# Routed experts on 256-row tiles of dispatched tokens instead of all tokens through every expert

## What is computed

```
x = x + _layernorm(attn(_layernorm(x)))          # 16 heads of 64, causal, relative bias
x = x + _layernorm(moe(_layernorm(x)))
# moe, xf is [2048, 128]:
shared = new_gelu(xf @ Wfc_s + bfc_s) @ Wproj_s + bproj_s        # 128 -> 512 -> 128
probs = softmax(xf @ Wr); topk_p, topk_i = top_k(probs, 2)
topk_p = topk_p / sum(topk_p)
for e in range(8):
    h = new_gelu(xf @ Wfc[e] + bfc[e]) @ Wproj[e] + bproj[e]
    routed = routed + h * gate[:, e:e + 1]                       # gate is 0 for 6 of 8 experts
```

## Time and profile before

| | |
|---|---|
| median of 3 runs | 844.47 us (841.37 to 845.34) |
| the profiled execution: its time | 844.46 us |
| its span | 842.7 us |
| PE busy | 771.5 us (92%) |
| DVE busy | 707.7 us (84%) |
| ACT busy | 612.8 us (73%) |
| POOL busy | 298.9 us (35%) |
| DMA moved | 70.72 MB |

### The profile page before, as it was taken

One profiled execution on the slowest core, in us unless ns is written; L12 is line 12 of the kernel. 1 busy time (PEld: TensorE's weight loads), 2 busy tenths in 40 slices (PEclk: granted clock), 3 DMA queues, 4 the chain that ended last, 5 costly groups with the idle time before them and its releaser, 6 DMA issues.

```text
span 842.7 us, 17198 instructions
## 1 busy us (share of the span) xinstructions
PE 771.5 (92%) x4436; PEld 657.1 (78%) x4436; DVE 707.7 (84%) x1596; ACT 612.8 (73%) x1340; POOL 298.9 (35%) x323
## 2 busy tenths in 40 slices
PE   3877999999999999999999999996489999999992
PEld 2656988888888888888889888885377777777771
DVE  5557888988888888888888888888778888898976
ACT  2356888887888888888788888873577767667672
POOL 2318823333332332333233233223503354445423
PEclk9899999999999999999999999999679999999997
DMA  7684334424423432442443343230003211122101
GB/s 279 219 280 89 75 66 97 88 62 87 100 62 76 95 77 62 93 94 62 87 95 67 70 97 82 62 75 26 25 1 129 76 60 43 46 75 75 51 1 50
DMA packets 56025, 70.72 MB, mean 84 GB/s; under 512 B 36032, under 2 KB 45120, under 8 KB 52544
## 3 DMA queue, kind: packets, MB, share of 16 engines
q1 hardware_dynamic: 55712, 69.83, 32.9%
q10 hardware_dynamic: 288, 0.59, 0.3%
HBM read 27.36 MB, written 9.50 MB: 44 GB/s over the span
## 4 chain that ended last, share of the span: by engine, by line
PE 75%; DVE 8%; issue 6%; POOL 4%; ACT 3%; DMA 3%; POOLq 0%; DVEq 0%; ACTq 0%; SPq 0%
PE out_ps L1191 16%; PE score_ps L1158 16%; PE trans_ps L1173 15%; PE shared_ps L1205 6%; PE trans_ps L1074 3%; PE score_ps L1074 3%; PE score_ps L1076 2%; PE score_ps L1075 2%; PE trans_ps L1075 2%; PE trans_ps L1076 2%; DVE pT_lo L961 2%; PE shared_ps L1074 2%; PE shared_ps L1076 2%; PE shared_ps L1075 2%; POOL rstd L421 1%
## 5 line engine op out<-in xcount | busy, mean ns | idle before, releaser
L649 ACT ACTIVATE probs<-score_ps,row_min 128x128 f32<-128x128 f32 (+7 forms) x256 | 189.9, 742 | 53.5 <-DVE row_min L848 53.4
L861 DVE TENSOR_TENSOR pT_lo<-trans_ps,pT_hi 128x512 fp32r<-128x512 f32 (+3 forms) x384 | 201.6, 552 | 16.7 <-ACT pT_hi L670 16.6
L670 ACT ACTIVATE pT_hi<-trans_ps 128x512 fp32r<-128x512 f32 (+3 forms) x384 | 185.1, 491 | 40.4 <-PE trans_ps L1173 28.8
L848 DVE CUSTOM_DVE_ANT_0 score_ps<-score_ps,bias 128x128 f32<-128x128 f32 (+7 forms) x256 | 194.6, 760 | 22.8 <-PE score_ps L1158 19.4
L1173 PE MATMUL trans_ps<-ident,probs 128*128 128x128 f32 x1152 | 190.0, 274 | 3.2 <-DVE pT_lo L861 1.8
L1158 PE MATMUL score_ps<-k_hl,q_hl 128*128 128x512 f32 (+2 forms) x768 | 182.5, 351 | 3.1 <-DMA k_hl<-k_hl 1.6
L470 POOL TENSOR_TENSOR acc<-acc,head_out 128x512 f32<-128x512 f32 x64 | 83.0, 1297 | 245.5 <-DVE head_out L879 245.3
L1173 PEld LDWEIGHTS trans_ps<-ident,probs 128*128 128x128 f32 x1152 | 136.8, 140 | 27.3 <-DVE pT_lo L861 11.9
L1191 PE MATMUL out_ps<-pT_hi,v_hl 128*128 128x512 f32 (+2 forms) x384 | 156.5, 409 | 1.1 <-DVE pT_lo L861 1.1
L961 DVE TENSOR_TENSOR pT_lo<-probs,pT_hi 128x512 fp32r<-128x512 f32 x144 | 133.2, 952 | 25.0 <-ACT pT_hi L728 15.1
L1158 PEld LDWEIGHTS score_ps<-k_hl,q_hl 128*128 128x128 f32 x768 | 134.4, 189 | 23.7 <-DMA k_hl<-k_hl 1.8
(11 more groups left out here) (122 smaller groups left out, 1163.3 us busy)
## 6 DMA issues: line engine op xcount, KB each, us to landing
q_hl<-k_hl SPq DMA_DIRECT2D x64, 256.0 KB, 3.6
k_hl<-k_hl SPq DMA_DIRECT2D x32, 512.0 KB, 4.2
v_scratch<-probs SPq DMA_DIRECT2D x16, 512.0 KB, 4.0
v_raw<-v_scratch SPq DMA_DIRECT2D x32, 256.0 KB, 4.6
bias_all<-gate_scratch SPq DMA_DIRECT2D x8, 1024.0 KB, 4.8
v_raw<-in_Wfc SPq DMA_DIRECT2D x8, 256.0 KB, 4.9
bias<-in_Wproj SPq DMA_DIRECT2D x8, 256.0 KB, 5.3
bias_all<-in_rel_steps SPq DMA_DIRECT2D x1, 1920.0 KB, 12.7
```

Source lines behind the costliest of these rows:

```text
L649: act.activation(probs[s % 4][:, 0:n], scores_of(s % QB)[:, 0:n], ACT.Exp, bias=row_min[:, s:s + 1], scale=-1.0, accum_out=row_sum[:, s:s ...
L670: act.activation(pT_hi[c][:, CH * g:CH * g + m, q * P:(q + 1) * P], trans_ps[k % 2][:, 0:m * P].rearrange("p (m q) -> p m q", q=P), ACT.Co ...
L848: dve.tensor_tensor_reduce(out=ps, in0=ps, in1=bias_b[b][:, T - n:T], scale=1.0, scalar=3e38, op0=ALU.add, op1=ALU.min, accum_out=row_min[ ...
L861: dve.tensor_tensor(pT_lo[c][dst], trans_ps[k % 2][:, 0:m * P].rearrange("p (m q) -> p m q", q=P), pT_hi[c][dst], ALU.subtract).then_inc(p ...
```

## The change

The routed experts no longer see all tokens. Each of the 2048 tokens has two picks, so there are 4096 rows of work. They are sorted by expert into a list in DRAM, in which each expert's part is padded to whole tiles of 256 rows (TS = 256, NJ = 2 blocks of 128). In the worst case that needs 23 tiles, NT = 23, and all 23 are always run.

- **Weights.** The 16 weight matrices of the routed experts ("halves") are split into high and low parts during the heads, one in each head: SP loads a half (256 KB), POOL splits it (`split_half`, in slot 10), SP stores both parts (512 KB) to `split_scratch`.
- **An emptied list.** During head 0 ACT's queue fills the 5888 rows of `rows_scratch` with zeros and with harmless destinations. POOL writes the small tables for it (`make_tables`).
- **Places.** PE counts with 17 small matmuls how many tokens before each one chose the same expert (`ranks`), and DVE works out from that the first tile of each expert and the slot of each row, with 14 small instructions.
- **Dispatch.** POOL scatters the token rows to their slots with 32 indirect DMAs of 128 rows (`dispatch`), each row of 130 numbers: 128 of the token, its gate, and where its result goes.
- **Tiles.** For each tile SP reads the tile's expert number from SBUF into a register, waits, issues two weight loads of 512 KB and one small one (`load_weights`), and loads rows of the tile three ahead of the weights (`load_rows`). There are three weight buffers, six row buffers and two result buffers. PE turns the rows (`tile_in`), runs twelve matmuls of 256 columns (`tile_units`), twelve more (`tile_second`), and turns the result back (`tile_result`). DVE scales by the gate, and POOL scatters the two blocks of the result to `y_scratch` with two indirect DMAs (`store_tile`).
- **End.** When all results have landed SP loads both parts of every token's result, DVE adds them to the shared expert's result, and the output norm goes as before.

The multiplications by three, the attention and the shared expert are as they were.

The core of the diff. SP, where it loads for the tiles:

```
+            def load_weights(i):
+
+                e = sp.value_load(tile_expert_i[0:1, i:i + 1], min_val=0, max_val=E - 1)
+                if i >= 3:
+                    sp.wait_ge(yT_ready, i - 2)
+                for part in range(2):
+                    sp.dma_start(tile_w[i % 3][part].bitcast(f32),
+                                 bass.AP(split_dram.tensor, e * (2 * P * 2 * HID) + part * (P * 2 * HID),
+                                         [[2 * HID, P], [1, 2 * HID]])).then_inc(tile_w_loaded[i % 3], 16)
...
+            def load_rows(i):
+
+                if i >= NR:
+                    sp.wait_ge(y_stored[(i - NR) % 2], 16 * NJ * ((i - NR) // 2 + 1))
+                sp.dma_start(tile_rows[i % NR], rows_dram[i * TS:(i + 1) * TS, :].rearrange("(j p) r -> p j r", p=P))\
+                  .then_inc(tile_rows_loaded[i % NR], 16)
...
+            sp.wait_ge(half_stored, 16 * HALVES)
+            sp.wait_ge(scores_ready, H * S)
+            sp.wait_ge(table_ready, 1)
+            for i in range(3):
+                load_weights(i)
+            sp.wait_ge(dispatched, 16 * 2 * NB)
+            for i in range(NR):
+                load_rows(i)
+            for i in range(3, NT):
+                load_weights(i)
+                if i + NR - 3 < NT:
+                    load_rows(i + NR - 3)
+
+            for i in (NT - 2, NT - 1):
+                sp.wait_ge(y_stored[i % 2], 16 * NJ * (i // 2 + 1))
+            for c in range(NCH):
+                for k in range(2):
+                    lo = k * B * T + c * W
+                    sp.dma_start(y_part[k][:, CH * c:CH * (c + 1), :],
+                                 y_dram[lo:lo + W, :].rearrange("(t p) d -> p t d", p=P)).then_inc(y_loaded[c], 16)
```

SP and POOL in the heads, and POOL's scatters:

```
+                store_half(h)
+                if not last:
+                    load_half(h + 1)
...
+                if s == QB + 2:
+                    split_half(h)
...
+            def dispatch():
+
+                pool.wait_ge(slots_ready, 1)
+                pool.wait_ge(fields_ready, 1)
+                pool.wait_ge(rows_emptied, 32)
+                for i in range(2):
+                    for t in range(NB):
+                        pool.indirect_dma_start(rows_dram, bass.IndirectOffsetOnAxis(slot_u[i][:, t:t + 1], 0),
+                                                rows[i][:, t, :], None).then_inc(dispatched, 16)
+
+            def store_tile(i):
+
+                pool.wait_ge(y_ready, i + 1)
+                for j in range(NJ):
+                    pool.indirect_dma_start(y_dram, bass.IndirectOffsetOnAxis(tile_rows[i % NR][:, j, D + 1:D + 2].bitcast(u32), 0),
+                                            tile_out[i % 2][:, j, :], None).then_inc(y_stored[i % 2], 16)
```

PE's tile loop, and DVE's:

```
+            tile_in(0)
+            for i in range(NT):
+                tile_units(i)
+                if i + 1 < NT:
+                    tile_in(i + 1)
+                if i:
+                    tile_second(i - 1)
+                if i >= 2:
+                    tile_result(i - 2)
...
+            tile_in(0)
+            for i in range(NT):
+                tile_units(i)
+                if i + 1 < NT:
+                    tile_in(i + 1)
+                if i >= 2:
+                    tile_result(i - 2)
```

More of the change, by code:

```diff
@@ L386, in _ @@
[L386 to L397, removed]
+            sp.dma_start(wfc_raw, Wfc_s).then_inc(moe_w_loaded, 16)
@@ L1012, in _ @@
             for i in range(2):
-                then_wait(dve.tensor_tensor(top[i][:], top[i][:], first[:], ALU.mult))
-                then_wait(dve.tensor_tensor(pick[i][:], pick[i][:], each(top[i][:]), ALU.mult))
-            dve.tensor_tensor(gate[:], pick[0][:], pick[1][:], ALU.add).then_inc(gate_ready, 1)
-            gate_expert(0, 0, 0)
+                last = dve.tensor_tensor(rows[i][:, :, D], top[i][:], first[:], ALU.mult)
+            last.then_inc(fields_ready, 1)
+            shared_out(0)
@@ new lines, in _ @@
+            dve.tensor_copy(tile_expert_i[:], tile_expert[:]).then_inc(table_ready, 1)
+            then_wait(dve.scalar_tensor_tensor(out=place[:], in0=first_tile[:].unsqueeze(1).broadcast_to([P, NB, E]),
+                                               scalar=float(TS), in1=shared_ps[:, 0:NB * E].rearrange("p (t e) -> p t e", e=E),
+                                               op0=ALU.mult, op1=ALU.add))
+            for i in range(2):
+                then_wait(dve.tensor_tensor(place_of[:], place[:], pick[i][:], ALU.mult))
+                then_wait(dve.tensor_reduce(slot_f[i][:], place_of[:], AX, ALU.add))
+                last = dve.tensor_copy(slot_u[i][:], slot_f[i][:])
@@ L1047, in add_x @@
+            tile_result(NT - 2)
+            tile_result(NT - 1)
+            def out_moments(c):
+                lo, hi = CH * c, CH * (c + 1)
+                dve.wait_ge(y_loaded[c], 32)
+                dve.wait_ge(shared_ready, NCH)
+                for k in range(2):
+                    then_wait(dve.tensor_tensor(acc[:, lo:hi, :], acc[:, lo:hi, :], y_part[k][:, lo:hi, :], ALU.add))
+                moments(acc, lo, hi)
             def add_x(c):
@@ L1305, in transpose_gates, with ranks @@
-            def transpose_gates():
-                pe.wait_ge(gate_ready, 1)
-                for c in range(NCH):
-                    last = pe.transpose(out_ps[0:CH * E, c * P:(c + 1) * P],
-                                        gate[:, CH * c:CH * (c + 1), :].rearrange("p j e -> p (j e)"), ident[:])
-                last.then_inc(gate_T_psum, 1)
+            def ranks():
+                pe.wait_ge(picks_ready, 1)
+                pe.wait_ge(tables_ready, 1)
+                width = (NB + 1) * E
+                pe.matmul(shared_ps[:, 0:width], before_me[:], taken[:], start=True, stop=False)
+                for d in range(1, NB + 1):
+                    last = pe.matmul(shared_ps[:, d * E:width], ones[:], taken[:, 0:width - d * E], start=False, stop=d == NB)
+                last.then_inc(rank_psum, 1)
@@ L1313, in _, with tile_result @@
+            def tile_result(i):
+                pe.wait_ge(yT_ready, i + 1)
+                if i:
+                    pe.wait_ge(y_ready, i)
+                else:
+                    pe.wait_ge(shared_ready, NCH)
+                for j in range(NJ):
+                    last = pe.transpose(shared_ps[:, j * P:(j + 1) * P], yT[i % 2][:, j * P:(j + 1) * P], ident[:])
+                last.then_inc(y_psum, 1)
             for c in range(NC):
```

473 lines of the change are left out of this document (302 added, 171 removed).

## The result

The changed kernel takes 909.2 us (median of 4 runs, 905.2 to 913.2) against 844.2 us (841.4 to 845.3): a ratio of 1.077, with an interval of 1.075 to 1.080. It is slower by 65 us. 897 were predicted, in a range of 846 to 932.

The account below looks back on a forecast made before the run. PE's columns bound the old kernel, SP's chain the new tiles. Slots at 639.0, first tile at 677.8, 176.2 us to tile 22 and the end gave 891.5; heads' 4 made 895.5, 897 us as a time, range 846 to 932.

Parts of the forecast that it names:

- The likeliest case: In the tiles, SP's chain of waits and loads sets the pace, 17.2 us per pair; time 850 to 930, chance 0.66.
- The rival of costly scatters: POOL is held, so dispatch and tile scatters cost 1.6 us or more each; time 925 and above, chance 0.14.
- Heads: ACT's two fills ahead of its first softmax cost 4 us, taken between 0 and 13; the other added work is hidden.
- the places: After the gates, PE's 17 small matmuls and DVE's 14 small instructions give the slots, ready at 639.0.
- heads no longer than before: A predicted sign in the attention heads: splitting, loading and storing weight halves there does not lengthen them.
- Dispatch and first tile: From the slots, 32 scatters of 1.0 us, landing and row loads last until 676.5; first tile at 677.8.
- Tiles: From the start of tile 0 to that of tile 22, 176.2 us, with pairs in the chain at 17.2 us.
- a full cold start: In each pair of tiles PE, after idling some 7 us, returns at half clock, adding 1.2 us.
- The free tiles at either end: Tiles outside SP's chain: 10.0 us from tile 0 to tile 2, and 11.4 us for tiles 21 and 22.
- Tile starts in pairs: A predicted sign in the tile stage: starts alternate about 5.5 and 11.7 us apart, 8.6 on average.
- From tile 22 to the span's end: Last tile, its scatters, result loads, additions and output norm run from 854.0 to 891.5.
- The faster rival: In the tiles, the chain on SP does not bind and tiles follow at 4.6 us; time 822, chance 0.13.

Follow-up runs that it names:

- e1: Against the changed kernel, SP's row loads run one tile ahead of the weight loads instead of three; 854.1 us (1.012).
- e6: Against the changed kernel, row loads one tile ahead and six whole-row fills in slots of the last head; 837.1 us (0.992).
- e5: Against the changed kernel, ACT's list fills become six DMAs of 520-byte rows, moved into slots of the last head; 901.6 us (1.068).
- e12: Against e7, 137 matmuls of 512 columns with unused results added on PE between shared expert and tile 0; 860.9 us (1.017).
- e9: Against e7, 110 matmuls of 512 columns with unused results added on PE between shared expert and tile 0; 833.0 us (0.987).
- e7: Against e6, PE counts ranks before chunk 1's second layer and DVE makes slots right behind the picks; 834.4 us (0.989).
- e8: Against the changed kernel, 32 more scatters of 64 rows behind the dispatch, into a second list nobody reads; 960.0 us in a single run.
- e4: Against the changed kernel, six DMAs of 520-byte rows replace ACT's two list fills, still ahead of head 0; 907.3 us (1.075).

## Why the prediction was right, and where its terms were off

**Direction and cause.** The likeliest case was the chain on SP, and it is what happened. e1 is the proof from one side: with the row load moved in SP's order and nothing else, 55 of the 65 us are gone. PE idle for some 30 us at the dispatch (34.8), waits ended by `split_scratch` (64.6 us in 19 waits, the largest 7.2), and tile starts above 6 us were all found. SP's wait for `y_stored` was 5.3 us a time and not 8. The rival of costly scatters is out: the 46 of the tiles are 0.965 us each on average, and the 32 of the dispatch 1.26 from start to start. The rule on POOL's descriptors (the Trainium skill, SBUF — State Buffer, section "SBUF: two separate sides"), by which they might have been 3.1 us, was not met in either stage. In the changed kernel it was hardly put to the test, as DVE did nothing during most scatters. In e6 15 of the tiles' scatters ran beside DVE's casts of L1208, and took 0.96 us all the same. The long ones of the changed kernel (1.51, 1.20 and 1.03 in the dispatch, 1.18 in the tiles) all ran beside DVE's work, so some hold by DVE is possible, but the largest is half of 3.1.

**The sum, term by term,** from its 895.5 to the profiled span of 903.1:

- **Heads: 4 was taken, 11.2 it was** (slots at 650.2, not 639.0). The heads cost 12.0 (PE's first count began at 644.5, where the gates were turned at 632.6), and the places took 5.7 from there and not 6.4. This step failed: "as most issues are short" I went low between 0 and 13. e5 gives 11.9 us back, and in the four other runs with the same code up to the slots they came 4.4 to 8.0 us later still. The statement "heads no longer than before" held from head 2 on, 32.5 us each in both kernels: the split, the store and the loads of halves are hidden. PE's one wait for k in the heads grew from 1.6 to 3.8 us.
- **Dispatch and first tile: 8.5 more.** I had 1.0 us for a scatter, which is its duration (0.96), and forgot the 0.30 between two. From start to start it is 1.26, and 32 with a slow first are 41.0 instead of 32. The rest gave some 0.5 back: 0.9 more from the slots to the first scatter and 0.4 more for the first tile, 0.9 less for the landing and 0.8 less for the rows.
- **Tiles: 10.1 less** (166.1 from tile 0 to tile 22, not 176.2). A pair was 15.9 instead of 17.2, nine times. The two scatters and the landing are 3.5 together and not 4.3, since the landing of 2.2 counts from the start of the second, and a full cold start came in only some of the turns. The table read is 0.8 (747.92 to 748.71), not 1.0. The Trainium skill, DMA: Bandwidth & Descriptors, section "Latency and other measured facts", has a floor of about 600 ns for a `tensor_load`. This trace does not agree: the load itself took 0.26 to 0.49 us, 0.27 as a rule, and the instruction behind it followed at once (733.26 and 733.56 in the chain above). The rest of the 0.8 is the two instructions that keep the number in bounds, and what stands between them. The free tiles at either end were 1.8 longer.
- **"Tile starts in pairs"** was right for e5 and only in part for the changed kernel, and the granted clock was at half at the start of one turn shown above and not of the other (0.21 and 0.12 us between matmuls). The mean of a pair is what counts for the sum.
- **From tile 22 to the span's end: 2 more.** Six scatters of the last three tiles stand in a row on POOL (+3.3), the loads are 0.3 longer, and the tail is 1.6 shorter (21.2 from the first addition to the end).

Together 11.2 + 8.5 - 10.1 + 3.3 + 0.3 - 1.6 = 11.6 on the 891.5 without heads. With the 4 that were taken for the heads, terms that were 19 too low met terms that were 12 too high. That the sum is right to 8 us (12 against the median, as the profiled execution is the shortest of the four) is in part luck.

**The faster rival was a near thing.** It gave 822 with 4.6 us per tile. With the lead of one and the fills out of the way the pace is 5.0, 10.0 for a pair, under the 11.3 at which I had the change break even, and the time is 837. What keeps it from 822 is the dispatch, 9 us longer than I had it, and the 4.7 to 6.1 us between tiles, in which the weights (DMA engines 0.75 to 0.84 busy, 254 to 282 GB/s in 700 to 780) still end PE's waits for 24.5 us.

**What stays open:** which limit holds ACT while it issues the fills, and whether place or spacing frees it; what chooses between the two rhythms of the slow chain; and what slowed PE in e12. That instructions came late is a guess. The DMA queues of kind "instruction" moved one packet between 650 and 661 us and the next only after 679. But in e9 they moved none from 650 to 679, and its matmuls ran on. POOL's last scatters and the row loads fall in the same time in both, so no run tells the cause.

## What to carry to other kernels

A load that waits for something late must not stand ahead of loads that could go: ask of every wait what is behind it on its queue, and what the engine that waits for that load has queued behind its own wait, for here two tiles less of lead gained 55 us and a third lost 77, and another buffer gained nothing. A long run of small DMAs is not free because it is issued early: spread out in a quiet stretch it held nobody up. With these mended, the design with 36% of the routed columns went from 7.7% slower to 1.1% faster. That is far from the 100 us that the columns promised: in e7 PE still idles for 28.9 us at the dispatch, and waits for weights for 26.0.

## What the runs showed of the hardware

- An indirect DMA of POOL costs 0.96 us for 128 rows and 0.90 for 64 (e8), plus 0.30 until the next. It was the same in the dispatch (DVE busy for 6.7 of 41 us) and in the tiles (DVE busy for 30 to 54% of the time). The last of a pair lands 2.2 us after its start. The first of the dispatch took 1.51, beside DVE's subtractions and a cast. The first of each pair in the tiles had no such surcharge.
- Issuing is not always short: a fill behind another one held ACT's instruction stream for 14.1 us at 50 us into the span. In e4, of six equal fills in a row, the first took 0.4 us and the others 1.5 to 4.0. The same six took 0.4 each when 2.5 to 4.5 us apart in the last head (e5).
- A straight run of equal matmuls without waits slowed for 17 us to one every 2 us or so (e12), with nothing in the profile to wait for. The cause is not known.
- A load of one number from SBUF into a register of SP took 0.27 us, and the whole read with its bounds 0.8, during which the queue issued nothing.
